# Four edits to the three cross-attention stages: the causal mask ahead of the scores, one eviction per half of P^T, the centring on ScalarE, the variance add on GpSimd

## The chip, the cores and the metric

One core of one Trainium2 chip. The metric is the device time of one execution in microseconds; lower is better. The program has one launch and no arithmetic on the host.

## The reference

The input x has 64 batches of 128 tokens by 128 features; a context has 77 tokens by 128 features for each batch. Four layers follow each other. The first three are cross-attentions with 16 heads of 8 features (the kernel calls them A0, A1 and A2); two of them have a feed-forward layer behind them (F0, F2). The fourth is self-attention with its own feed-forward layer (A3, F3). A cross-attention layer computes, for each batch:

```
q = x @ Wq (+ bq);  k = ctx @ Wk (+ bk);  v = ctx @ Wv (+ bv)      # 128x128, 77x128, 77x128
s[h] = q[h] @ k[h]^T                                              # 16 heads of 128x77
A0: s += -1e9 where key > query          (causal)
A1: s = s * side[h];  s += -3e38 where mask[h]    (weights and a mask of 128x77 a head, from DRAM)
A2: s += -1e20 where the key's mask is 0
p = softmax(s * scale);  o = p @ v;  t = x + o (A0) or x + o @ Wo + bo (A1, A2)
y = (t - mean(t)) / sqrt(var(t) + 1e-5) * gamma + beta
```

## The kernel before

**Stages and loops.** The stages run one after the other in the order A0, F0, A1, A2, F2, A3, F3 and hand their results over in DRAM. In A0, A1 and A2 each engine runs a loop of its own over the 64 batches, unrolled four times, and the engines meet through semaphores only. In one step of the loop an engine works on several batches at once: in step b it does the scores of batch b+1, the transposes and exponentials of batch b, the output of batch b-1, and the layer norm of batches b-2 and b-3. The order inside a step is written by hand, and an engine does its instructions strictly in that order; nothing overtakes a waiting one.

**A step on TensorE** (function `step` of `cross_tensor`): `scores(b+1)` (L659: four fp32 products over 32 rows each, for four heads at a time, into PSUM banks 0 to 3); in A0 then eight bf16 products that add the causal mask, each with a 64x64 corner of the identity as one operand (L667), in A2 four that add the key mask from `keybias` (L673). Then `attend(b-1)` (L702), `transpose_p(b, 0)` (L685: eight transposes of 128x77, four into bank 4 and four into bank 5), `back(b-1)` (L716), the projections of keys, values and queries of later batches (L639, L642, L633), the transpose of x (L629), and `transpose_p(b, 1)` (L685 again, into the same banks 4 and 5, so it waits until the first half was evicted). The projected keys and values share banks 0 and 1 with the scores (columns from 308 on).

**A step on ScalarE**: `keep_att` (L819), in A1 the exponential of the second half (L766), `keep_pT(b, 0)` (L772: two evictions of 77x512, one for each bank, each with its own semaphore count), the eviction of the keys (L781 in A0, L779 in A2; in A1 four that build the blocked keys directly, L787), of values, queries (L806) and x transposed (L794), an exponential (L766), `keep_pT(b, 1)` (L772 twice), an exponential.

**A step on VectorE** in A0 and A2: the row maxima of the scores (L863) and the subtraction (L868), for two halves; the mean and variance of batch b-3 (L943) between the first two; then the normalised output (L916, L923), the sum with the residual (L935), in A2 the key mask of batch b+2 (L906), and the statistics (L939). In A1 (`step_weighted`): the product of scores and weights for both halves (L876), the variance add of batch b-3 (L947), the mask of half 0 (L881), 1/denominator, the maxima of half 0 (L889), the normalised output, the values, the sum (L935), the mask of half 1 (L881), the statistics, the maxima of half 1 (L889), mean and variance (L943).

**A step on GpSimd** in A0 and A2: variance add (L1021), power -1/2 (L1026), the residual with bias (L1017), the centring and scaling z = (t - mean) * rstd (L1030), the blocked keys of batch b+2 (L1004), gamma (L1035) and beta (L1038). In A1: the subtraction of the maximum for half 1 of batch b (L1009), the power (L1026), the residual (L1017), the centring (L1030), the subtraction for half 0 of batch b+1 (L1009), gamma (L1035), beta (L1038).

SyncE alone issues DMAs. The tensors `p`, `kblk`, `att` and `side` are cut out of one large SBUF tensor, which the profile calls `sb_region`.

Of the kernel before, what the change touches and what calls it, by code (L numbers as in the profile page):

```python
# [29 lines left out]
T = 128  # L30
D = 128
C = 77
# [106 lines left out]
def build_layers(nc, a, out):  # L139
# [3 lines left out]
    with ExitStack() as ctx:  # L143
# [31 lines left out]
        causal = sb("causal", [T, 2 * C], BF16)  # L175
# [116 lines left out]
        rstd_s = slots("rstd", [T, 1])  # L292
        z_s = slots("z", [T, D])
# [49 lines left out]
        causal32, tri32 = wvo[:, 0:2 * C], wvo[:, 512:512 + HC * SEG]  # L343
        causal_loads = []
        for r in range(2):
            both = a["c_causal"].rearrange("(g i) (h k) -> i g h k", g=2, k=C)
            causal_loads.append((causal32[r * KH:(r + 1) * KH, :].rearrange("p (g k) -> p g k", k=C), both[:, :, 0, :]))
# [60 lines left out]
        pT_made = event("pT_made", CROSS, parts=4)  # L408
        pT_kept = event("pT_kept", CROSS, parts=4)
# [12 lines left out]
        rstd_made = event("rstd_made", CROSS)  # L422
        z_made = event("z_made", CROSS)
# [190 lines left out]
        def cross_tensor(pe, ph):  # L614
# [28 lines left out]

            def scores(b):
                if ph == "A0" and b.first:
                    pe.wait_ge(masks_made, 3)
# [8 lines left out]
                if (b + -1).exists:  # L655
                    pe.wait_ge(taken.sem(b + -1), taken.count(ph, b + -1, 1))
                for c in range(NQ):
                    rows = slice(32 * c, 32 * c + 32)
                    mm = nc.tensor.matmul(bank[c][:, 0:QC], qT_s[b.par][rows, :], kblk_s[b.par][rows, :],  # L659
                                          start=True, stop=(ph == "A1"), skip_group_check=(ph == "A0"))  # L660
                if ph == "A0":
                    for c in range(NQ):
                        for g in range(2):
                            r = (g + c) % 2
                            rows = slice(r * KH, (r + 1) * KH)
                            later = causal[rows, g * C:(g + 1) * C].unsqueeze(1).to_broadcast([KH, QH, C])
                            mm = nc.tensor.matmul(bank[c][g * KH:(g + 1) * KH, 0:QC], identb[rows, r * KH:(r + 1) * KH], later,  # L667
                                                  start=False, stop=True, skip_group_check=True)
# [1468 lines left out]
```

## Time and profile before

| what | value |
| --- | --- |
| time, median of 3 runs | 2447.12 us (2447.01 to 2448.53) |
| the profiled execution: time, span | 2447.01 us, 2445.2 us |
| TensorE / VectorE / GpSimd / ScalarE busy, share of the span | 93% / 77% / 64% / 62% |
| A0, first to last scores | 9.7 to 353.9 us |
| A1, first to last power | 543.8 to 922.7 us |
| A2, first to last key mask | 921.8 to 1271.1 us |

The profiled execution agrees with the median to 0.1 us. The span is what the trace covers; 1.8 us of the time lie around it. The three cross-attention stages have 192 steps in all. The page's shares are means over stages that have different limits, so the steady part of each stage is shown apart among the rows below.

### The profile page before, as it was taken

To read this page: it belongs to the slowest core of one execution; us is meant where nothing else is said; L and a number is where in the kernel's file an instruction comes from. 1 tells how busy PE (TensorE), PEld (TensorE's weight loads), DVE (VectorE), ACT (ScalarE), POOL (GpSimd) and SP (SyncE) were. 2 spreads that over 40 slices of the span, in tenths; PEclk is the share of its full clock that TensorE was granted. 3 is DMA by queue.
4 is the path that set the end of the run, shared out by engine and by line. 5 is a ranking of instruction groups with operands and counts; after the bars stand their busy time and mean duration, and the time that the engine had idled before them with its cause. 6 is when DMAs were issued, how large, how long until landed. Compare 5 with 4: busy or idle time off the path is not lost.

```text
span 2445.2 us, 84677 instructions
## 1 busy us (share of the span) xinstructions
PE 2268.4 (93%) x27182; PEld 1803.6 (74%) x27182; DVE 1876.9 (77%) x4067; ACT 1509.1 (62%) x3728; POOL 1555.4 (64%) x2374
## 2 busy tenths in 40 slices
PE   7999999988888888999999979999999999999899
PEld 5777778966666666777778867777777777777677
DVE  5888871159999986777775678888888888888565
ACT  5888884558888886888884524444444444444433
POOL 2666662229999994666667766666666666666332
PEclk9999999979999998999999999999999999999999
DMA  4111112235555542222221233333333333333111
GB/s 128 45 45 44 45 45 64 82 103 168 167 167 166 166 130 53 50 50 51 50 48 58 70 79 93 95 96 96 96 95 94 94 94 94 95 94 92 51 58 54
DMA packets 443189, 211.73 MB, mean 87 GB/s; under 512 B 206672, under 2 KB 434000, under 8 KB 442960
## 3 DMA queue, kind: packets, MB, share of 16 engines
q1 hardware_dynamic: 443088, 210.43, 31.9%
q8 instruction: 57, 0.93, 0.2%
q14 instruction: 44, 0.36, 0.1%
HBM read 113.28 MB, written 29.88 MB: 59 GB/s over the span
## 4 chain that ended last, share of the span: by engine, by line
PE 51%; POOL 18%; issue 16%; DVE 8%; SPq 3%; DMA 2%; ACT 1%; POOLq 1%; DVEq 0%; ACTq 0%
PE bank L1457 9%; PE bank L1417 9%; PE bank L1148 5%; POOL sb_region L1009 4%; PE bank L1485 4%; PE bank L659 4%; PE bank L1162 4%; POOL sb_rstd L1026 4%; POOL sb_z L1030 3%; PE bank L1467 3%; PE bank L1443 3%; DVE sb_max L863 2%; PE bank L685 2%; PE bank L1493 2%; POOL sb_region L1004 1%
## 5 line engine op out<-in xcount | busy, mean ns | idle before, releaser
L772 ACT ACTIVATE sb_pT<-bank 77x512 f32<-77x512 f32 x768 | 413.1, 591 | 19.5 <-PE bank L685 13.2
L685 PE MATMUL bank<-sb_ident,sb_region 128*77 128x128 f32 x3072 | 412.8, 278 | 5.3 <-ACT sb_pT L772 3.0
L685 PEld LDWEIGHTS bank<-sb_ident,sb_region 128*77 128x77 f32 x3072 | 355.1, 151 | 32.6 <-issue 14.4
L1547 ACT ACTIVATE sb_l<-sb_l 128x640 f32<-128x640 f32 x128 | 94.4, 738 | 388.0 <-DVE sb_l L1595 388.0
L863 DVE TENSOR_REDUCE sb_max<-bank 128x8 f32<-128x616 f32 x256 | 203.5, 795 | 128.5 <-PE bank L673 65.9
L766 ACT ACTIVATE sb_region<-sb_region 128x616 f32<-128x616 f32 x384 | 277.7, 724 | 21.3 <-POOL sb_region L1009 21.0
L1674 POOL TENSOR_TENSOR sb_pn<-sb_l,sb_r_all 128x512 f32<-128x512 f32 x128 | 134.7, 1052 | 234.2 <-DVE sb_r_all L1605 226.2
L1417 PE MATMUL bank<-sb_region,sb_wqkv 128*128 128x128 f32 x2048 | 253.3, 277 | 5.8 <-DVE sb_region L1583 5.0
L659 PE MATMUL bank<-sb_region,sb_qT 32*128 32x308 f32 x1536 | 158.1, 481 | 100.6 <-ACT sb_region L787 37.9
L1457 PE MATMUL bank<-sb_wvo,sb_region 128*64 128x512 f32 x1024 | 247.9, 605 | 0.0
L1417 PEld LDWEIGHTS bank<-sb_region,sb_wqkv 128*128 128x128 f32 x2048 | 241.7, 194 | 8.2 <-DVE sb_region L1583 5.7
L868 DVE TENSOR_TENSOR sb_region<-bank,sb_max 128x616 f32<-128x616 f32 x256 | 204.8, 800 | 18.5
L702 PE MATMUL bank<-sb_pT,sb_v 77*32 77x128 f32 x6144 | 209.0, 276 | 1.8 <-ACT sb_pT L772 1.8
L1665 POOL TENSOR_TENSOR sb_region<-sb_region 128x512 f32<-128x512 f32 x128 | 162.5, 1269 | 71.7 <-PE bank L1443 62.8
L702 PEld LDWEIGHTS bank<-sb_pT,sb_v 77*32 77x32 f32 x6144 | 155.7, 109 | 70.3 <-issue 57.2
L1009 POOL TENSOR_TENSOR sb_region<-sb_region,sb_max 128x616 f32<-128x616 f32 x128 | 174.5, 1364 | 37.0 <-DVE sb_max L889 37.0
L1485 PEld LDWEIGHTS bank<-sb_region,sb_pT 128*64 128x64 f32 x2048 | 121.6, 137 | 79.3 <-issue 67.3
L1197 ACT ACTIVATE sb_fh<-bank,sb_L_xattn_ffb 128x256 f32<-128x256 f32 x256 | 109.0, 472 | 112.6 <-PE bank L1148 112.6
L1531 ACT ACTIVATE sb_region<-bank 128x512 f32<-128x512 f32 x256 | 150.9, 592 | 40.1 <-PE bank L1457 31.0
L1583 DVE TENSOR_TENSOR sb_region<-bank,sb_sinT 128x512 f32<-128x512 f32 x256 | 174.3, 681 | 0.0
L1583 DVE TENSOR_TENSOR sb_region<-bank,sb_cosT 128x512 f32<-128x512 f32 x256 | 172.7, 675 | 1.4 <-PE bank L1417 1.3
L659 PEld LDWEIGHTS bank<-sb_region,sb_qT 32*128 32x128 f32 x1536 | 63.0, 187 | 144.2 <-issue 123.8
(181 smaller groups left out, 5531.9 us busy)
## 6 DMA issues: line engine op xcount, KB each, us to landing
sb_region<-in_side SPq DMA_DIRECT2D x64, 616.0 KB, 3.8
sb_pT<-sb_region SPq DMA_DIRECT2D x512, 64.0 KB, 2.0
sb_kF<-sb_region SPq DMA_DIRECT2D x512, 64.0 KB, 2.1
scratch_after_A<-sb_y SPq DMA_DIRECT2D x256, 64.0 KB, 1.8
sb_fx<-scratch_after_A SPq DMA_DIRECT2D x96, 128.0 KB, 2.1
sb_mask<-in_mask SPq DMA_DIRECT2D x64, 154.0 KB, 2.3
sb_x<-scratch_after_F SPq DMA_DIRECT2D x128, 64.0 KB, 1.9
sb_ctx<-in_ctxT SPq DMA_DIRECT2D x192, 38.5 KB, 1.8
```

Of the source, the lines that this page charges most:

```text
L659: mm = nc.tensor.matmul(bank[c][:, 0:QC], qT_s[b.par][rows, :], kblk_s[b.par][rows, :], start=True, stop=(ph == "A1"), skip_group_check=(p ...
L685: mm = nc.tensor.transpose(bank[4 + q][0:C, h * T:(h + 1) * T], p_s[b.par][:, head * C:(head + 1) * C], ident[:])
L702: mm = nc.tensor.matmul(att_bank[32 * i:32 * i + 32, k * T:(k + 1) * T], v_s[b.par][:, first:first + 32], pT_s[k][:, h * T:(h + 1) * T], s ...
L766: nc.scalar.activation(half(p_s[b.par], k), half(p_s[b.par], k), ACT.Exp, scale=SCALE[ph]).then_inc(exp_made.sem(b), 1)
L772: nc.scalar.activation(pT_s[k][:, q * QH * T:(q + 1) * QH * T], bank[4 + q][0:C, :], ACT.Copy).then_inc(pT_kept.sem(b), 1)
L863: nc.vector.tensor_reduce(dst, by_bank_and_head(scores_half(k)), AX.X, ALU.max).then_inc(max_made.sem(b), 1)
L868: nc.vector.tensor_tensor(by_bank_and_head(by_bank(half(p_s[b.par], k))), by_bank_and_head(scores_half(k)), spread_max(k), ALU.subtract).t ...
L1009: nc.gpsimd.tensor_tensor(by_head(half(p_s[b.par], k)), by_head(half(p_s[b.par], k)), spread(max_s[:, 8 * k:8 * k + 8], C), ALU.subtract)\
L1417: mm = nc.tensor.matmul(rope_bank[eo][:, n * T:(n + 1) * T], wqkv[:, col:col + 128], xnT_s[b.lap], start=True, stop=True)
L1457: mm = nc.tensor.matmul(vo_banks[g][r * SEG:(r + 1) * SEG, :], xnT_s[b.lap][:, g * SEG:(g + 1) * SEG], wvo[:, (2 * h + r) * HC * D:(2 * h ...
L1485: nc.tensor.matmul(out3_bank[g * SEG:(g + 1) * SEG, 0:D], pT_s3[h][:, c * T + g * SEG:c * T + (g + 1) * SEG], vo_s[h][:, (g * HC + c) * D: ...
L1583: ins = nc.vector.tensor_tensor(part[what][eo].rearrange("p (n t) -> p n t", t=T), src, table[:].unsqueeze(1).to_broadcast([128, BLOCKS, T ...
```

## The change

- **Causal mask (A0).** The mask tile grows from two 77-column blocks in 64-row parts to the full 128x308. The eight corner products behind the scores go. Four products of the full 128x128 identity with the full mask stand ahead of the scores in their PSUM banks (`start=True`), and the scores accumulate onto them. Those of banks 0 and 1 are issued at the end of the step before (`mask_early`), after waiting until the keys and values that share these banks were evicted; those of banks 2 and 3 stand right ahead of the scores, behind their waits.
- **P^T (A0, A1, A2).** The two evictions of 77x512 become one of 77x1024, over both banks. It waits for all eight transposes, and the second half's transposes wait for the whole of it.
- **Layer norm (A1).** VectorE's variance add (L947) goes; GpSimd does it (as in A0 and A2). GpSimd's centring goes; in its place GpSimd makes -mean * rstd of 128x1 (`scale_mean`), and ScalarE does z = t * rstd + shift of 128x128 between `keep_xT` and `keep_pT(b, 1)`.
- **Loads.** The causal mask is loaded by one DMA in place of two.

```diff
-        causal = sb("causal", [T, 2 * C], BF16)
+        causal = sb("causal", [T, QC], BF16)
...
+        shift_s = slots("mean_shift", [T, 1])
...
-        pT_made = event("pT_made", CROSS, parts=4)
-        pT_kept = event("pT_kept", CROSS, parts=4)
+        pT_made = event("pT_made", CROSS, parts=2)
+        pT_kept = event("pT_kept", CROSS, parts=2)
...
+            def mask_early(b, values):
+                if b.first:
+                    pe.wait_ge(masks_made, 3)
+                pe.wait_ge(k_kept.sem(b), k_kept.count(ph, b))
+                if values:
+                    pe.wait_ge(v_kept.sem(values), v_kept.count(ph, values))
+                for c in range(2):
+                    nc.tensor.matmul(bank[c][:, 0:QC], identb[:], causal[:], start=True, stop=False)
...
+                if ph == "A0":
+                    for c in range(2, NQ):
+                        nc.tensor.matmul(bank[c][:, 0:QC], identb[:], causal[:], start=True, stop=False)
                 for c in range(NQ):
                     rows = slice(32 * c, 32 * c + 32)
                     mm = nc.tensor.matmul(bank[c][:, 0:QC], qT_s[b.par][rows, :], kblk_s[b.par][rows, :],
-                                          start=True, stop=(ph == "A1"), skip_group_check=(ph == "A0"))
-                if ph == "A0":
-                    for c in range(NQ):
-                        for g in range(2):
-                            r = (g + c) % 2
-                            rows = slice(r * KH, (r + 1) * KH)
-                            later = causal[rows, g * C:(g + 1) * C].unsqueeze(1).to_broadcast([KH, QH, C])
-                            mm = nc.tensor.matmul(bank[c][g * KH:(g + 1) * KH, 0:QC], identb[rows, r * KH:(r + 1) * KH], later,
-                                                  start=False, stop=True, skip_group_check=True)
+                                          start=(ph != "A0"), stop=(ph != "A2"))
...
             def transpose_p(b, k):
                 pe.wait_ge(exp_made.sem(b), exp_made.count(ph, b, k))
-                for q in range(2):
-
-                    old, old_k = (b, 0) if k == 1 else (b + -1, 1)
-                    if old.exists:
-                        pe.wait_ge(pT_kept.sem(old), pT_kept.count(ph, old, 2 * old_k + q))
-                    for h in range(QH):
-                        head = (2 * k + q) * QH + h
-                        mm = nc.tensor.transpose(bank[4 + q][0:C, h * T:(h + 1) * T], p_s[b.par][:, head * C:(head + 1) * C], ident[:])
-                    mm.then_inc(pT_made.sem(b), 1)
+
+                if k == 1:
+                    pe.wait_ge(pT_kept.sem(b), pT_kept.count(ph, b, 0))
+                elif (b + -1).exists:
+                    pe.wait_ge(pT_kept.sem(b + -1), pT_kept.count(ph, b + -1, 1))
+                for h in range(2 * QH):
+                    head = k * 2 * QH + h
+                    mm = nc.tensor.transpose(two[0:C, h * T:(h + 1) * T], p_s[b.par][:, head * C:(head + 1) * C], ident[:])
+                mm.then_inc(pT_made.sem(b), 1)
...
                 if has(0):
                     transpose_p(b, 1)
+                if has(2) and ph == "A0":
+                    mask_early(b + 2, b + 1 if has(1) else None)
...
             def keep_pT(b, k):
+                act.wait_ge(pT_made.sem(b), pT_made.count(ph, b, k))
                 wait_earlier(act, att_made, ph, b, 1, k)
-                for q in range(2):
-                    act.wait_ge(pT_made.sem(b), pT_made.count(ph, b, 2 * k + q))
-                    nc.scalar.activation(pT_s[k][:, q * QH * T:(q + 1) * QH * T], bank[4 + q][0:C, :], ACT.Copy).then_inc(pT_kept.sem(b), 1)
+                nc.scalar.activation(pT_s[k][:], two[0:C, :], ACT.Copy).then_inc(pT_kept.sem(b), 1)
...
+            def centre(b):
+                act.wait_ge(mean_scaled.sem(b), mean_scaled.count(ph, b))
+                wait_earlier(act, zg_made, ph, b, 2)
+                nc.scalar.activation(z_s[b.par][:], t_s[b.par][:], ACT.Identity, bias=shift_s[b.par][:, 0:1], scale=rstd_s[b.par][:, 0:1])\
+                    .then_inc(z_made.sem(b), 1)
...
                     keep_xT(b + 3)
+                if has(-3) and weighted:
+                    centre(b + -3)
                 if has(1) and not weighted:
                     exps(b + 1, 0)
...
-                if has(-3):
-                    variance(b + -3)
-                if has(1):
                     mask(b + 1, 0)
...
+            def scale_mean(b):
+
+                nc.gpsimd.tensor_scalar(shift_s[b.par][:], mv_s[b.par][:, 0:1], rstd_s[b.par][:, 0:1], -1.0, ALU.mult, ALU.mult)\
+                    .then_inc(mean_scaled.sem(b), 1)
...
                     if has(-3):
-                        root(b + -3)
+                        rstd(b + -3)
+                        wait_earlier(pool, z_made, ph, b + -3, 2)
                     if has(-1):
                         residual(b + -1)
                     if has(-3):
-                        centre(b + -3)
+                        scale_mean(b + -3)
```

## Rows read from the trace of the kernel before

**Rows 1.** Busy time by stretch (steady A0, A1, A2): length, then PE, PEld, DVE, ACT, POOL.
```profile
99.58:322.45 222.87, 212.70 (x3066) 166.68 (x3067) 184.81 (x421) 189.38 (x464) 148.70 (x295) 1.00 0.17 45
570.00:880.00 310.00, 259.13 (x3409) 207.38 (x3412) 285.64 (x655) 273.58 (x707) 293.04 (x352) 1.00 0.57 167
963.82:1249.73 285.91, 266.63 (x3744) 221.96 (x3745) 226.62 (x521) 244.98 (x625) 183.97 (x365) 1.00 0.23 50
```
**Rows 2.** Timeline of a step of A0: start, length, engine, line, operation, [idle before <-releaser].
```profile
181.20 1.10 PE L685 MATMUL bank<-sb_ident,sb_region 128*77 128x128 f32 x8
181.90 1.08 ACT L772 ACTIVATE sb_pT<-bank 77x512 f32<-77x512 f32 x2 [0.18 <-PE bank L685]
182.98 0.91 PEld L685 LDWEIGHTS bank<-sb_ident,sb_region 128*77 128x77 f32 x8
...
183.53 0.70 POOL L1004 TENSOR_TENSOR sb_region<-sb_kT,sb_rowmask 128x308 f32<-128x308 f32 x1
184.46 0.80 PE L659 MATMUL bank<-sb_region,sb_qT 32*128 32x308 f32 x8 [0.33 <-POOL sb_region L1004]
185.19 0.47 PE L667 MATMUL bank<-sb_causal,sb_identb 64*64 64x308 bf16 x8
185.59 1.08 PE L702 MATMUL bank<-sb_pT,sb_v 77*32 77x128 f32 x32
```
**Rows 3.** Groups by line over the span: busy us, mean ns of one, idle before.
```profile
L772 ACT ACTIVATE sb_pT<-bank 77x512 f32<-77x512 f32 x768 | 413.1, 591 | 19.5 <-PE bank L685 13.2
L819 ACT ACTIVATE sb_region<-bank 128x256 f32<-128x256 f32 x192 | 73.6, 383 | 108.3 <-PE bank L702 108.3
L1021 POOL TENSOR_TENSOR sb_var<-sb_mv,sb_ln_eps 128x1 f32<-128x1 f32 x128 | 24.6, 192 | 183.8 <-DVE sb_mv L943 183.8
```
**Rows 4.** Timeline of a step of A1.
```profile
702.52 1.21 POOL L1009 TENSOR_TENSOR sb_region<-sb_region,sb_max 128x616 f32<-128x616 f32 x1
703.61 0.79 DVE L881 SCALAR_TENSOR_TENSOR sb_region<-sb_mask,sb_region 128x616 f32<-128x616 uint8 x1
703.76 0.72 ACT L766 ACTIVATE sb_region<-sb_region 128x616 f32<-128x616 f32 x1 [0.26 <-POOL sb_region L1009]
703.78 1.05 POOL L1026 TENSOR_TENSOR sb_rstd<-sb_var,sb_minus_half 128x1 f32<-128x1 f32 x1
705.49 0.80 POOL L1030 TENSOR_SCALAR sb_z<-sb_t,sb_mv,sb_rstd 128x128 f32<-128x128 f32 x1
705.91 0.79 DVE L881 SCALAR_TENSOR_TENSOR sb_region<-sb_mask,sb_region 128x616 f32<-128x616 uint8 x1
706.26 1.51 POOL L1009 TENSOR_TENSOR sb_region<-sb_region,sb_max 128x616 f32<-128x616 f32 x1
707.02 0.80 DVE L889 TENSOR_REDUCE sb_max<-sb_region 128x8 f32<-128x616 f32 x1
708.68 1.21 POOL L1009 TENSOR_TENSOR sb_region<-sb_region,sb_max 128x616 f32<-128x616 f32 x1
```
**Rows 5.** Instructions of line 1026: duration ns min/median/max, first and last start.
```profile
L1026 POOL TENSOR_TENSOR sb_rstd<-sb_var,sb_minus_half x192: 557/560/1123, 38.8 to 1289.2; 128x1 f32<-128x1 f32 x192
```
**Rows 6.** Timeline of VectorE and GpSimd at the start of A1.
```profile
533.29 1.22 POOL L1009 TENSOR_TENSOR sb_region<-sb_region,sb_max 128x616 f32<-128x616 f32 x1 [2.38 <-DVE sb_max L889]
533.52 1.65 DVE L881 SCALAR_TENSOR_TENSOR sb_region<-sb_mask,sb_region 128x616 f32<-128x616 uint8 x1
```
**Rows 7.** Timeline of a step of A2.
```profile
1103.30 1.04 PE L685 MATMUL bank<-sb_ident,sb_region 128*77 128x128 f32 x8
1104.99 0.24 ACT L779 ACTIVATE sb_kT<-bank 128x77 f32<-128x77 f32 x1
1105.46 0.70 POOL L1004 TENSOR_TENSOR sb_region<-sb_kT,sb_rowmask 128x308 f32<-128x308 f32 x1
1106.12 0.46 POOL L1035 TENSOR_TENSOR sb_zg<-sb_z,sb_L_xattn_ln_g 128x128 f32<-128x128 f32 x1
1106.19 0.44 DVE L906 TENSOR_SCALAR sb_keybias<-sb_keymask 128x77 bf16<-128x77 int32 x1
```

More of the change, by code:

```diff
@@ L341, in build_layers @@
         persK = sb("persK", [128, H // 2, NPM])
[L343 to L347, printed above, removed]
+        causal32, tri32 = wvo[:, 0:QC], wvo[:, 512:512 + HC * SEG]
+        causal_loads = [(causal32, a["c_causal"])]
         consts.append((tri32, a["c_tri"]))
@@ L422, in build_layers @@
         rstd_made = event("rstd_made", CROSS)
+        mean_scaled = event("mean_scaled", ["A1"])
         z_made = event("z_made", CROSS)
@@ L642, in project_values @@
                 nc.tensor.matmul(v_bank[0:C, V_COL:V_COL + D], ctx_s[b.par][:], w["wv"][:], start=True, stop=True).then_inc(v_made.sem(b), 1)
+            def mask_early(b, values):
[6 more added lines that the diff above has]
+                    nc.tensor.matmul(bank[c][:, 0:QC], identb[:], causal[:], start=True, stop=False)
             def scores(b):
-                if ph == "A0" and b.first:
-                    pe.wait_ge(masks_made, 3)
                 pe.wait_ge(kblk_made.sem(b), kblk_made.count(ph, b))
@@ L677, in transpose_p @@
                 pe.wait_ge(exp_made.sem(b), exp_made.count(ph, b, k))
[L678 to L686 removed]
+                if k == 1:
[6 more added lines that the diff above has]
+                mm.then_inc(pT_made.sem(b), 1)
             def attend(b, k, columns=None):
[L689 removed]
+                pe.wait_ge(pT_kept.sem(b), pT_kept.count(ph, b, k))
                 if k == 0:
@@ L856, in half_free @@
             def half_free(b, k):
-                wait_earlier(dve, pT_made, ph, b, 2, 2 * k + 1)
+                wait_earlier(dve, pT_made, ph, b, 2, k)
             def peak(b, k):
@@ L943, in aggregate @@
                 nc.vector.bn_aggr(mv_s[b.par][:], stats_s[b.par][:]).then_inc(mv_made.sem(b), 1)
-            def variance(b):
-                dve.wait_ge(mv_made.sem(b), mv_made.count(ph, b))
-                nc.vector.tensor_scalar(var_s[b.par][:], mv_s[b.par][:, 1:2], LN_EPS, None, ALU.add).then_inc(var_made.sem(b), 1)
             def step_weighted(b, has):
@@ L1021, in rstd @@
                 nc.gpsimd.tensor_tensor(var_s[b.par][:], mv_s[b.par][:, 1:2], ln_eps[:, 0:1], ALU.add).then_inc(var_made.sem(b), 1)
-                root(b)
-            def root(b):
                 pool.wait_ge(var_made.sem(b), var_made.count(ph, b))
@@ L2007, in _ @@
             nc.vector.tensor_copy(identb[:], ident[:]).then_inc(masks_made, 1)
-            dve.wait_ge(causal_loaded, 2 * 16)
+            dve.wait_ge(causal_loaded, 1 * 16)
             nc.vector.tensor_copy(causal[:], causal32).then_inc(masks_made, 1)
```

1 line of the change is left out of this document (removed).

## The prediction

> **What bounds the kernel now.** The page comes first, for the stages and the shares, then the busy time by stretch, then the timeline of one step of each stage, and last the groups by line for durations. Only A0, A1 and A2 run changed code, 64 steps each. In the stretches [rows 1] GpSimd has seven instructions in a step, so they hold 295/7 = 42, 352/7 = 50 and 365/7 = 52 steps, and a step takes 222.87/42 = 5.31 us in A0, 310/50.3 = 6.17 in A1 and 285.91/52 = 5.50 in A2. The reader is to see there that no stage is simply full: TensorE is 95% busy in A0, GpSimd 95% in A1, and in A2 TensorE shows 93% and VectorE 79%. The timeline tells what closes each step.
>
> In A0 the scores start 0.23 us after the blocked keys are done (184.46 against 183.53 + 0.70) and TensorE had stood idle for 0.33 by then [rows 2]. The loop is scores, mask, maxima, statistics, GpSimd's chain to the blocked keys, scores. TensorE's own work is close behind it.
>
> In A1 GpSimd looks full, but part of that is waiting. Its power takes 0.56 us at the median of the kernel and 1.05 here; its subtraction takes 1.21 at 702.52 and 1.51 at 706.26 [rows 4, 5]. Each long one lies over VectorE's mask (L881), and each ends a fixed time behind it: the power 0.43 after the mask that ends at 704.40, the subtraction 1.07 after the one that ends at 706.70. The other way round, a mask issued at 533.52 inside a subtraction that ends at 534.51 takes 1.65 and ends 0.66 after it [rows 6]. So these two kinds of instruction exclude each other, and who is issued first goes first. Written as a loop with M the end of the first mask: subtraction of half 1 ends 703.73, M = 704.40 (+0.67), second mask issued M+1.51, ended M+2.30, subtraction of half 0 ends M+3.37, gamma, beta and the next half-1 subtraction end 709.89 = M+5.49. 0.67 + 5.49 = 6.16, the step. The centring (0.80 at 705.49) is not in it: it lies beside the normalised output on VectorE and ends at 706.29, before the second mask lets go at 706.70.
>
> In A2 the scores wait for the key mask (L906), which ends at 1106.63, itself stretched to 0.44 over GpSimd's gamma product (1106.12 to 1106.58) [rows 7]. The blocked keys were done at 1106.16.
>
> **The change part by part: one eviction of P^T.** The evictions of 256 and 512 columns take 383 and 591 ns [rows 3], 0.81 ns a column, so 1024 columns take an estimated 1.01 us. Two evictions back to back take 1.08 [rows 2], so ScalarE gains 0.07 a half, which it doesn't need: it is busy 85 to 88% [rows 1]. Bounds for the new one are 0.90 and 1.08. What counts is when it starts and ends. With T the start of the first half's transposes (181.20), the first eviction starts at T+0.70, four transposes in; the other four take half of 0.91 more, so the joined one starts at T+1.16 and ends at T+2.17. The second half's transposes now wait for that and start at T+2.20, where they started at T+1.78.
>
> **A0.** TensorE's chain becomes: wait to T+2.20; eight transposes to the next instruction 1.0 (0.91 of weight loads and the first product's start); four full mask products; scores 0.73 (184.46 to 185.19); attend 1.0 to the next T. The old chain checks it: 184.46 + 0.73 + 0.40 + 1.01 gives 186.60, 5.40 after 181.20, in a step a little longer than the mean. A full bf16 product of 308 columns has no row. The eight corner products take 0.40, four of them at most side by side, so one round is 0.05 to 0.20; I take 0.13 each, 0.52 for four, and 0.40 to 0.80 as bounds. The sum is 2.20 + 1.0 + 0.52 + 0.73 + 1.01 = 5.46 against 5.31: +0.15 a step, **+10 us** over 64. The loop through the blocked keys does get shorter: only two products (0.26) stand between keys and scores where 0.40 stood behind them, so 5.31 - 0.14 = 5.17, but TensorE no longer reaches it. The keys' eviction (0.24 by A2's row [rows 7]) now ends near T+2.4, so the blocked keys run T+2.5 to T+3.2, 0.2 later than now; TensorE has its transposes and first two products behind it only at T+3.46. `mask_early` waits for keys and values that ScalarE evicts right behind T+2.17, before TensorE gets there at T+3.20: nothing. With both ends of the unknown costs A0 goes from -2 to +28; the upper end needs every product at its worst, so +18 is the end I keep.
>
> **A1.** VectorE loses its variance add, GpSimd loses 0.80 and gains a variance add (0.19 [rows 3]), a 128x1 product (about 0.2, by the same row) and their gaps. The first mask is still held until the half-1 subtraction ends, so M stays at +0.67, and VectorE's way from M to M+2.30 is untouched. GpSimd now does behind M: the rest of the variance add (0.1), the power 0.56, residual and gaps 0.66 (704.83 to 705.49 [rows 4]), the product 0.2: it issues the half-0 subtraction at M+1.5, where the second mask is issued at M+1.51. If the mask is first, the subtraction still ends at M+3.37 and the step stays 6.16: the freed 0.3 to 0.4 us turns into waiting for the mask. If the subtraction is first, it ends at M+2.71, the mask ends 0.66 behind it at M+3.37, the maxima at M+4.49 (1.12 behind the mask, 706.70 to 707.82), the next half-1 subtraction at M+5.77: the step is 6.44, +0.27. I take a third of the steps so: 21 x 0.27 = **+5 us**, with 0 and +17 as bounds. ScalarE's centring (370 ns at most, a 256-column copy takes 383 [rows 3]) stands behind the query eviction, where ScalarE has 12% free [rows 1] and gamma comes 1.5 us later; joined evictions pay for 0.14 of it: nothing. What is queued behind it, the second half's eviction and an exponential, moves by 0.2 and has a step's time to be used.
>
> The Trainium skill (SBUF — State Buffer, section on the two separate sides) says the SBUF port pair that VectorE and GpSimd share is an exclusive lock, taken for a whole instruction by whichever starts first, for a VectorE instruction with two SBUF inputs. The trace agrees: 1.65 us for a mask of 0.79 [rows 6]. By a rule of shared bandwidth instead, the centring's 0.80 would come off the step in part, and A1 would gain.
>
> **A2.** Here only the eviction changes. T is 1103.30; the joined eviction runs from T+1.16 to T+2.17 = 1105.47, the keys' eviction (0.24) ends near 1105.6 where it ended at 1105.23, the blocked keys run 1105.68 to 1106.38 where they ran 1105.46 to 1106.16. Scores at 1106.77 leave 0.2 for that. The key mask issued at 1106.19 then meets the blocked keys, not gamma, and gets through at 1106.45 in place of 1106.63: -0.18 where it goes so. In steps in which it is issued later it meets gamma, which is 0.2 later itself. I take -0.1 a step, **-6 us**; bounds are -11 and, if gamma always gets ahead of it, +12.
>
> Layer norm code elsewhere is untouched, and one larger mask load at the start (158 KB in place of twice 39) lies before the first scores: under 1 us, left out. The sum against the profiled execution (2447.0, 0.1 under the median): 2447 + 10 + 5 - 6 = **2456 us**.
>
> **The rivals.** (a) A1 is set free: GpSimd's 0.80 counts in full. Then ScalarE's chain bounds the step; its wait for the half-1 subtraction is 0.26 [rows 4], so at most 0.26 x 64 = 17 us come off: 2447 - 17 + 10 - 6 = 2434. For it speaks GpSimd's 95%; against it the subtraction's end 1.07 behind the mask. It decides when the half-0 subtraction ends well before M+3.3. (b) The second half's transposes aren't late, or the full mask products cost under 0.1 each, and A0 closes over the blocked keys at 5.17: -9, sum 2447 - 9 + 5 - 6 = 2437. Against it stands the start at T+2.20. (c) The subtraction wins every time in A1: 2447 + 10 + 17 - 6 = 2468. (d) A2's key mask doesn't profit, or is stuck behind gamma: 2447 + 10 + 5 + 0 to 12 = 2462 to 2474. (e) The edits cancel, A0's loss at half its size: 2450.
>
> **How the numbers follow.** Under 0.2% (4.9 us) a measurement can't tell this kernel from no change. Chances: forecast (2452 to 2461) 0.38; (a) 0.14; (b) 0.13; (c) 0.10; (d) 0.10; (e) 0.15. Faster by over 0.2%: (a) and nearly all of (b), 0.26. Within: (e) and the edges of (b) and of the forecast, 0.18. Slower: the rest, 0.56. The range takes 2436 to 2470: it leaves out most of (a) and the end of (d). The forecast's own range is 2452 to 2461.
>
> **What would show it.** In the new profile: one eviction of 77x1024 near 1.0 us; transposes of the second half 2.2 us behind those of the first in A0; no wait of TensorE for blocked keys there; a step of 5.46. In A1 power no longer stretched but the variance add is (to 0.7), masks of over 1.2 us in some steps, a step of 6.16 to 6.44. In A2 a key mask that ends right behind the blocked keys. The prediction is wrong if A1's step falls under 6.0, if TensorE still waits for the blocked keys in A0, or if A2's scores come to wait for them.

## The result and the profile after

The changed kernel takes 2475.32 us (2472.53 to 2476.01, 4 runs) against 2447.14 (2447.01 to 2448.53, 4 runs): the ratio is 1.0111, with a 95% interval of 1.0094 to 1.013. It is slower, as forecast, but by 28 us where 9 were forecast, and outside the range.

The span went from 2445.2 to 2470.1 us in the profiled execution, which took 2471.87 us, 3.4 less than the median. The starts of the scores say where the 24.9 us are. The table gives the mean step in us over 40 steps in the middle of each stage, taken between the starts of the scores on TensorE. The experiments below are in it too. The steps come from one profiled execution of each kernel, the ratios from all its timed ones.

| kernel | A0 | A1 | A2 | ratio to before (95%) |
| --- | --- | --- | --- | --- |
| before | 5.31 | 6.17 | 5.50 | |
| changed | 5.59 | 6.33 | 5.42 | 1.0111 (1.0094 to 1.013) |
| mask edit only | 5.30 | 6.18 | 5.50 | 1.0005 (0.9995 to 1.0015) |
| joined eviction only | 5.52 | 6.16 | 5.41 | 1.0040 (1.0025 to 1.0055) |
| norm edits only | 5.31 | 6.34 | 5.51 | 1.0058 (1.0038 to 1.0078) |
| changed, two evictions again | 5.29 | 6.33 | 5.51 | 1.0045 (1.0027 to 1.0062) |
| norm edits, product on VectorE | 5.31 | 6.24 | 5.50 | 1.0013 (1.0001 to 1.0025) |
| before, late blocked keys in A2 | 5.32 | 6.17 | 5.44 | 0.9992 (0.9975 to 1.0009) |
| before, four masks early | 5.12 | 6.17 | 5.50 | 0.9952 (0.9935 to 0.997) |
| before, other GpSimd order in A1 | 5.31 | 6.14 | 5.50 | 0.9992 (0.9982 to 1.0002) |
| changed, four masks early | 5.58 | 6.33 | 5.41 | 1.0108 (1.0093 to 1.0124) |
| combined | 5.12 | 6.18 | 5.45 | 0.9957 (0.9943 to 0.9971) |

From first to last scores (63 steps) A0 got 16.9 us longer (344.1 to 361.0), A1 8.2 (387.8 to 396.0), A2 3.9 shorter (345.9 to 342.0). The stretches between the stages, which hold the tail of one and the head of the next, add 2.3 (F0) and 1.3 (between A1 and A2). The sum is 24.8, the rest is at the two ends. By the ratios, the mask edit alone (+0.05%), the joined eviction alone (+0.40%) and the norm edits alone (+0.58%) add up to +1.03%, close to the +1.11% of the whole.

Busy time by stretch of the changed kernel, steady A0, A1 and A2, for [rows 1]; the columns are the same:

```profile
99.00:322.00 223.00, 212.29 (x2758) 165.08 (x2757) 177.18 (x401) 172.22 (x359) 143.68 (x280) 1.00 0.16 42
570.00:880.00 310.00, 260.13 (x3335) 200.16 (x3335) 291.87 (x591) 279.57 (x639) 287.40 (x393) 1.00 0.55 163
960.00:1250.00 290.00, 284.25 (x3826) 227.02 (x3827) 227.07 (x524) 235.71 (x531) 181.04 (x357) 0.99 0.24 52
```

In A1 GpSimd's busy share fell only from 95% to 93%, and VectorE's rose from 92% to 94%, although GpSimd lost 0.80 us of centring a step and VectorE lost an instruction: both now hold instructions that are stretched. In A2 TensorE went from 93% to 98%.

**A0, a step of the changed kernel**, timeline, for [rows 2]:

```profile
182.21 1.10 PE L686 MATMUL bank<-sb_ident,sb_region 128*77 128x128 f32 x8
...
183.35 1.02 ACT L774 ACTIVATE sb_pT<-bank 77x1024 f32<-77x1024 f32 x1 [0.54 <-PE bank L686]
...
184.51 1.07 PE L686 MATMUL bank<-sb_ident,sb_region 128*77 128x128 f32 x8 [0.25 <-ACT sb_pT L774]
...
184.66 0.70 POOL L1007 TENSOR_TENSOR sb_region<-sb_kT,sb_rowmask 128x308 f32<-128x308 f32 x1 [0.21 <-ACT sb_kT L783]
...
185.42 0.42 PE L650 MATMUL bank<-sb_causal,sb_identb 128*128 128x308 bf16 x2
...
185.68 0.42 PE L665 MATMUL bank<-sb_causal,sb_identb 128*128 128x308 bf16 x2
...
186.03 0.80 PE L668 MATMUL bank<-sb_region,sb_qT 32*128 32x308 f32 x8
...
```

T, the start of the first half's transposes, is 182.21. The joined eviction runs from T+1.14 to T+2.16, the second half's transposes start at T+2.30, and TensorE names the eviction as what it waited for. In the kernel before, the last products ahead of them and the transposes were these:

```profile
182.98 0.27 PE L629 MATMUL bank<-sb_ident,sb_x 128*128 128x128 f32 x1
183.09 1.04 PE L685 MATMUL bank<-sb_ident,sb_region 128*77 128x128 f32 x8
```

There T is 181.20. The transposes stood at T+1.89, right behind the work in front of them and with no wait: the two evictions had begun with four transposes still to come and had both ended by T+1.78 [rows 2]. In the changed kernel the four mask products take 0.61 (185.42 to 186.03). The blocked keys are done at 185.36, and TensorE shows no wait for them any more.

**A1**, a step of the changed kernel, for [rows 4]:

```profile
707.02 0.75 POOL L1024 TENSOR_TENSOR sb_var<-sb_mv,sb_ln_eps 128x1 f32<-128x1 f32 x1
707.85 0.55 POOL L1026 TENSOR_TENSOR sb_rstd<-sb_var,sb_minus_half 128x1 f32<-128x1 f32 x1
708.72 0.45 POOL L1020 TENSOR_TENSOR sb_xb<-sb_xr,sb_L_xattn_bo 128x128 f32<-128x128 f32 x1 [0.32 <-POOL sb_rstd L1026]
709.15 0.91 POOL L1035 TENSOR_SCALAR sb_mean_shift<-sb_mv,sb_rstd 128x1 f32<-128x1 f32 x1
710.03 1.21 POOL L1012 TENSOR_TENSOR sb_region<-sb_region,sb_max 128x616 f32<-128x616 f32 x1
```
```profile
706.71 1.01 DVE L891 SCALAR_TENSOR_TENSOR sb_region<-sb_mask,sb_region 128x616 f32<-128x616 uint8 x1
...
709.15 0.79 DVE L891 SCALAR_TENSOR_TENSOR sb_region<-sb_mask,sb_region 128x616 f32<-128x616 uint8 x1
```

The variance add takes 0.75 in place of 0.19 [rows 3] and ends 0.05 behind the first mask (707.72). The product of one element a partition, issued at 709.15 with the second mask, takes 0.91 and ends 0.12 behind it. The half-0 subtraction is no longer stretched, but it starts only then and ends 1.30 behind the mask where it ended 1.07 behind it. With M the end of the first mask, as in the prediction, its end is M+3.52 in place of M+3.37.

**A2**, a step of the changed kernel, for [rows 7]:

```profile
1115.20 1.02 ACT L774 ACTIVATE sb_pT<-bank 77x1024 f32<-77x1024 f32 x1 [0.47 <-PE bank L686]
...
1116.36 1.07 PE L686 MATMUL bank<-sb_ident,sb_region 128*77 128x128 f32 x8
1116.50 0.70 POOL L1007 TENSOR_TENSOR sb_region<-sb_kT,sb_rowmask 128x308 f32<-128x308 f32 x1 [0.34 <-ACT sb_kT L781]
1116.84 0.42 DVE L916 TENSOR_SCALAR sb_keybias<-sb_keymask 128x77 bf16<-128x77 int32 x1
...
1117.47 0.80 PE L668 MATMUL bank<-sb_region,sb_qT 32*128 32x308 f32 x8
```

The key mask is stretched over the blocked keys and gets through 0.06 behind them. The scores start with no wait for it shown, right behind the second half's transposes. Those start 0.14 behind the joined eviction (1116.22), so that in this stage too TensorE now follows the eviction.

### The profile page after: what moved, and what is told of

Its sections match the earlier page's. It is cut to its first block, busy times and chain, and to the rows that moved or that the text cites. A ratio compares the mean times of both kernels' runs of the same rounds, so it can differ in the third digit from the quotient of the medians.

```text
span 2470.1 us, 83369 instructions
## 1 busy us (share of the span) xinstructions
PE 2308.8 (93%) x26926; PEld 1812.7 (73%) x26926; DVE 1888.0 (76%) x4003; ACT 1498.6 (61%) x3408; POOL 1559.2 (63%) x2438
## 4 chain that ended last, share of the span: by engine, by line
PE 68%; POOL 16%; issue 6%; ACT 3%; DVE 3%; DMA 2%; SPq 1%; POOLq 1%; DVEq 0%; ACTq 0%
PE bank L686 10%; PE bank L1463 9%; PE bank L1423 9%; POOL sb_region L1012 5%; PE bank L703 5%; PE bank L1491 5%; PE bank L1154 4%; PE bank L668 4%; PE bank L1168 4%; PE bank L1473 3%; PE bank L1449 3%; ACT sb_pT L774 3%; POOL sb_mean_shift L1035 2%; POOL sb_var L1024 2%; PE bank L1499 2%
## 5 line engine op out<-in xcount | busy, mean ns | idle before, releaser
L774 ACT ACTIVATE sb_pT<-bank 77x1024 f32<-77x1024 f32 x384 | 391.6, 1020 | 81.4 <-PE bank L686 80.4
L686 PEld LDWEIGHTS bank<-sb_ident,sb_region 128*77 128x77 f32 x3072 | 348.3, 151 | 112.1 <-issue 108.2
L769 ACT ACTIVATE sb_region<-sb_region 128x616 f32<-128x616 f32 x384 | 276.9, 722 | 25.0 <-POOL sb_region L1012 24.9
L703 PE MATMUL bank<-sb_pT,sb_v 77*32 77x128 f32 x6144 | 216.2, 277 | 3.8 <-ACT sb_pT L774 3.6
L1012 POOL TENSOR_TENSOR sb_region<-sb_region,sb_max 128x616 f32<-128x616 f32 x128 | 158.8, 1241 | 37.5 <-DVE sb_max L899 37.5
L1024 POOL TENSOR_TENSOR sb_var<-sb_mv,sb_ln_eps 128x1 f32<-128x1 f32 x192 | 68.0, 354 | 174.8 <-DVE sb_mv L953 174.8
```

What stands on the lines that cost most here:

```text
L686: mm = nc.tensor.transpose(two[0:C, h * T:(h + 1) * T], p_s[b.par][:, head * C:(head + 1) * C], ident[:])
L703: mm = nc.tensor.matmul(att_bank[32 * i:32 * i + 32, k * T:(k + 1) * T], v_s[b.par][:, first:first + 32], pT_s[k][:, h * T:(h + 1) * T], s ...
L769: nc.scalar.activation(half(p_s[b.par], k), half(p_s[b.par], k), ACT.Exp, scale=SCALE[ph]).then_inc(exp_made.sem(b), 1)
L774: nc.scalar.activation(pT_s[k][:], two[0:C, :], ACT.Copy).then_inc(pT_kept.sem(b), 1)
L1012: nc.gpsimd.tensor_tensor(by_head(half(p_s[b.par], k)), by_head(half(p_s[b.par], k)), spread(max_s[:, 8 * k:8 * k + 8], C), ALU.subtract)\
```

## The experiments

**Mask edit only.** The kernel before with the causal-mask part of the diff.

```diff
+                for c in range(2):       # mask_early, end of the step before
+                    nc.tensor.matmul(bank[c][:, 0:QC], identb[:], causal[:], start=True, stop=False)
...
+                    for c in range(2, NQ):       # in scores, behind its waits
+                        nc.tensor.matmul(bank[c][:, 0:QC], identb[:], causal[:], start=True, stop=False)
```

> The kernel before with the causal-mask edit alone (A0). Theory: A0's loss in the changed kernel comes from the second half's transposes starting 0.5 us late, and the four full mask products (0.61 us in the changed kernel, 0.40 for the eight corner products) hurt only because they stand behind that delay. Alone, the mask edit takes 0.14 us out of the loop through the blocked keys and leaves TensorE's chain at 1.78 + 0.91 + 0.11 + 0.61 + 0.73 + 1.01 = 5.15: A0 at 5.15 to 5.2 us a step against 5.31, the whole at 2438 to 2441. Rival: the mask products themselves are what slows A0; then this kernel has most of the 0.27 us a step, some 2460.

Measured: 2449.3 against 2448.41 us, ratio 1.0005; A0 at 5.30. The rival falls: the mask edit doesn't slow A0. The expected gain isn't there either. Timeline of a step:

```profile
182.78 0.70 POOL L1005 TENSOR_TENSOR sb_region<-sb_kT,sb_rowmask 128x308 f32<-128x308 f32 x1
...
183.19 0.42 PE L648 MATMUL bank<-sb_causal,sb_identb 128*128 128x308 bf16 x2
...
183.71 0.43 PE L663 MATMUL bank<-sb_causal,sb_identb 128*128 128x308 bf16 x2
...
184.07 0.80 PE L666 MATMUL bank<-sb_region,sb_qT 32*128 32x308 f32 x8
...
184.94 0.80 DVE L864 TENSOR_REDUCE sb_max<-bank 128x8 f32<-128x616 f32 x1 [0.97 <-PE bank L666]
```

From the end of the blocked keys (183.48) to the maxima it is 1.46 us. In the kernel before, the blocked keys end at 184.23 [rows 2], and the maxima start 1.47 later:

```profile
185.70 0.80 DVE L863 TENSOR_REDUCE sb_max<-bank 128x8 f32<-128x616 f32 x1 [0.98 <-PE bank L667]
```

The two late full products take 0.36 (183.71 to 184.07), and the maxima start 0.87 behind the start of the scores, which are now last. Before, the scores took 0.73 until the corner products, and the maxima started 0.51 behind the start of those. 0.36 + 0.87 is 1.23, 0.73 + 0.51 is 1.24. Nothing is gained.

**Joined eviction only.** The kernel before with one eviction of 77x1024.

```diff
-                for q in range(2):
-                    act.wait_ge(pT_made.sem(b), pT_made.count(ph, b, 2 * k + q))
-                    nc.scalar.activation(pT_s[k][:, q * QH * T:(q + 1) * QH * T], bank[4 + q][0:C, :], ACT.Copy)...
+                act.wait_ge(pT_made.sem(b), pT_made.count(ph, b, k))
+                nc.scalar.activation(pT_s[k][:], two[0:C, :], ACT.Copy)...
```

> The kernel before with the joined eviction alone (A0, A1, A2). Theory: A0 takes 5.40 to 5.50 a step (the blocked keys are 0.1 to 0.2 later and the corner masks still stand behind the scores), +6 to +12 us; A1 is unchanged, because GpSimd and the masks on VectorE close its step; A2 falls to 5.42 as in the changed kernel, -5 us. Sum 2448 to 2454. Rival: A1's extra 0.16 us a step is the joined eviction's too; then A1 is at 6.33 and the sum is 10 us higher, 2458 to 2464.

Measured: 2457.24 against 2448.41 us, ratio 1.0040; A0 5.52, A1 6.16, A2 5.41. The rival falls: A1's loss isn't the eviction's. A0 loses 0.21 a step here already, a little more than the 0.10 to 0.20 expected. All of A2's gain is here. In A0 the mask edit, which costs nothing alone, adds 0.07 a step to this (5.52 to 5.59 in the changed kernel): there the two edits do interact. TensorE's chain is the longer one once the eviction is late, and four full mask products take 0.61 in it where the corner products took 0.40, while the transposes take 0.91 to the next instruction in place of 1.00.

**Norm edits only.** The kernel before with A1's layer-norm edits.

```diff
-                    variance(b + -3)              # VectorE
...
-                        centre(b + -3)            # GpSimd
+                        rstd(b + -3)              # GpSimd, with the variance add
...
+                        scale_mean(b + -3)        # GpSimd, 128x1
...
+                    centre(b + -3)                # ScalarE
```

> The kernel before with the layer-norm edits of A1 alone. Theory: all of A1's loss is here (half-0 subtraction on GpSimd getting in ahead of the second mask on VectorE): A1 at 6.3 us a step against 6.17, +8 to +12 us, 2456 to 2459; A0 and A2 as before. Rival 1: the loss is the joined eviction's, and this kernel is at 2447 or below. Rival 2: GpSimd's freed time counts without the longer eviction, and A1 falls under 6.1: 2440.

Measured: 2459.92 against 2448.41 us, ratio 1.0058; A1 at 6.34, A0 and A2 as before. All of A1's loss is here. How it comes about differs between the start of A1 and its steady part. At the start, GpSimd and then VectorE:

```profile
540.86 0.26 POOL L1035 TENSOR_SCALAR sb_mean_shift<-sb_mv,sb_rstd 128x1 f32<-128x1 f32 x1
541.08 1.21 POOL L1012 TENSOR_TENSOR sb_region<-sb_region,sb_max 128x616 f32<-128x616 f32 x1
```
```profile
541.27 1.68 DVE L891 SCALAR_TENSOR_TENSOR sb_region<-sb_mask,sb_region 128x616 f32<-128x616 uint8 x1
```

The product takes 0.26, the subtraction gets in ahead of the mask, and the mask takes 1.68. The next half-1 subtractions start at 544.06 and 550.30: a step of 6.24. From the fifth product on (566.21) to the one at 882.81, it is the product that waits for the mask, with 0.91 to 1.08 us each, at 6.34 a step. One of them, GpSimd and then VectorE:

```profile
705.44 1.04 POOL L1035 TENSOR_SCALAR sb_mean_shift<-sb_mv,sb_rstd 128x1 f32<-128x1 f32 x1
706.44 1.21 POOL L1012 TENSOR_TENSOR sb_region<-sb_region,sb_max 128x616 f32<-128x616 f32 x1
```
```profile
705.64 0.79 DVE L891 SCALAR_TENSOR_TENSOR sb_region<-sb_mask,sb_region 128x616 f32<-128x616 uint8 x1
```

The product starts 0.20 before the mask in the records, and still ends 0.05 behind it, while the mask keeps its 0.79. So for this pair the record that starts first is not the one that goes first. In this trace every product that starts 0.25 us or more ahead of the mask takes 0.25 to 0.27, and each one that starts up to 0.24 ahead of it waits. The prediction had only the first of the two outcomes as a loss, and took the second for free.

**The changed kernel with two evictions.** Everything but the joined eviction.

```diff
-                act.wait_ge(pT_made.sem(b), pT_made.count(ph, b, k))
...
-                nc.scalar.activation(pT_s[k][:], two[0:C, :], ACT.Copy).then_inc(pT_kept.sem(b), 1)
+                for q in range(2):
+                    act.wait_ge(pT_made.sem(b), pT_made.count(ph, b, 2 * k + q))
+                    nc.scalar.activation(pT_s[k][:, q * QH * T:(q + 1) * QH * T], bank[4 + q][0:C, :], ACT.Copy)...
```

> The changed kernel with P^T evicted in two halves again. Theory: the parts add up by stage: A0 as with the mask alone (5.15 to 5.2), A1 as with the norm edits alone (6.3), A2 as before (5.50): 2447 - 7 + 10 = 2450. Rival: the edits interact in A1 (the centring on ScalarE hurts only beside the longer eviction), and this kernel is at 2440.

Measured: 2458.06 against 2448.41 us, ratio 1.0045 (+10 us where +3 was expected by sum); A0 5.29, A1 6.33, A2 5.51. Stage by stage it is the mask-only and the norm-only kernel side by side, so the edits don't interact in A1. Its time is 8 us above the expected 2450. The expectation had 7 us for a gain of the mask edit, and that gain isn't there. In the trace the stretches between stages are also longer than in the kernel before (behind A0 164.1 against 162.7 us, behind A1 23.2 against 21.6), but that execution took 2465.91 us, the longest of four, so this is only an indication.

**Norm edits with the product on VectorE.** The diff is against the kernel with the norm edits only.

```diff
-                        scale_mean(b + -3)        # GpSimd, between residual and subtraction
+                if has(-3):
+                    scale_mean(b + -3)            # VectorE, between values and sum
```

> The norm edits of A1 alone, with the 128x1 product of mean and rstd made by VectorE (between the values and the sum) and not by GpSimd. In the norm-only kernel that product is issued on GpSimd within 0.05 us of VectorE's second mask, loses, takes 0.9 to 1.1 us in place of 0.26, and the half-0 subtraction starts only behind it, 0.1 behind the mask's end, with its full 1.21. Theory: A1's step is set by the turns that masks and GpSimd's two-input instructions take. Without the product GpSimd issues the subtraction ahead of the mask, the mask is stretched to about 1.65, and the step is 6.2 to 6.25, as in the first steps of A1 in the norm-only kernel (6.24): still not under 6.17, although GpSimd now does 0.8 us less than before. Rival: A1's loss is the product's 0.7 us of GpSimd time; without it A1 falls under 6.1.

Measured: 2452.6 against 2448.54 us, ratio 1.0013; A1 at 6.24. A step of GpSimd and then VectorE at 700 us:

```profile
700.39 1.22 POOL L1020 TENSOR_TENSOR sb_region<-sb_region,sb_max 128x616 f32<-128x616 f32 x1
702.30 0.45 POOL L1043 TENSOR_TENSOR sb_zg<-sb_z,sb_L_xattn_ln_g 128x128 f32<-128x128 f32 x1 [0.70 <-ACT sb_z L820]
```
```profile
700.94 1.32 DVE L891 SCALAR_TENSOR_TENSOR sb_region<-sb_mask,sb_region 128x616 f32<-128x616 uint8 x1
```

The subtraction is first now (700.39 against 700.94) and the mask takes 1.32. GpSimd stands idle for 0.70 us before gamma, and the stage is still not faster than with the whole centring on GpSimd. The rival falls: GpSimd's work was not what bound A1. Of the 0.17 a step that the norm edits cost, 0.10 goes with the product's place on GpSimd. Which of the other norm edits costs the remaining 0.07 was not tried apart.

**Late blocked keys in A2.** Nothing is removed; a wait is added.

```diff
+                if ph == "A2" and (b + -1).exists:       # block_keys, GpSimd
+                    pool.wait_ge(v_kept.sem(b + -1), v_kept.count(ph, b + -1))
```

> The kernel before; only in A2 GpSimd's blocked keys wait for the values' eviction too, which delays them by about 0.15 us and removes nothing. Theory: A2's gain in the changed kernel (5.50 to 5.41 a step) comes from the blocked keys being late, so that VectorE's key mask meets them and not the gamma product, and gets through right behind them. Then the late keys alone bring A2 to 5.35 to 5.43. Rival: the gain is ScalarE's, from one eviction in place of two; then this kernel stays at 5.50 or gets slower.

Measured: 2444.84 against 2448.54 us, ratio 0.9992, an interval that includes 1; A2 at 5.44 against 5.50, just outside what was expected and on the theory's side. Timeline of GpSimd, VectorE and TensorE:

```profile
1104.93 0.70 POOL L1006 TENSOR_TENSOR sb_region<-sb_kT,sb_rowmask 128x308 f32<-128x308 f32 x1 [0.22 <-ACT sb_v L813]
1105.41 0.28 DVE L906 TENSOR_SCALAR sb_keybias<-sb_keymask 128x77 bf16<-128x77 int32 x1
1105.86 0.80 PE L659 MATMUL bank<-sb_region,sb_qT 32*128 32x308 f32 x8 [0.25 <-DVE sb_keybias L906]
```

The key mask gets through 0.06 behind the blocked keys. The stage gets 0.06 us a step shorter by a wait alone; the joined eviction alone has 0.09. So the late keys account for most of A2's gain; that they account for all of it isn't shown.

**Four masks early.** The kernel before with all four mask products in `mask_early`. The diff is against the kernel with the mask edit only.

```diff
+                if values:
+                    pe.wait_ge(taken.sem(values), taken.count(ph, values, 1))
-                for c in range(2):
+                for c in range(NQ):
                     nc.tensor.matmul(bank[c][:, 0:QC], identb[:], causal[:], start=True, stop=False)
...
-                    for c in range(2, NQ):       # in scores
-                        nc.tensor.matmul(bank[c][:, 0:QC], identb[:], causal[:], start=True, stop=False)
```

> The kernel before with all four full causal-mask products of A0 at the end of the step before (the mask-only kernel has two of them there and two behind the wait for the blocked keys). Theory: the mask-only kernel gained nothing (5.30 a step) because its two late products cost 0.36 us and the scores' tail 0.07 between the blocked keys and the maxima, against 0.40 for the eight corner products. With all four early that is gone from the loop, and TensorE's own chain binds: 0.73 + 1.01 + 1.03 + 0.95 + 0.87 + 0.52 = 5.11: A0 at 5.1 to 5.15, -10 to -12 us. Rival: full mask products slow TensorE itself; then A0 stays at 5.3 or rises.

Measured: 2439.1 against 2448.54 us, ratio 0.9952 (0.9935 to 0.997): faster by 9.4 us where 10 to 12 were expected; A0 at 5.12. Timeline of TensorE:

```profile
182.68 1.10 PE L683 MATMUL bank<-sb_ident,sb_region 128*77 128x128 f32 x8
...
184.57 1.04 PE L683 MATMUL bank<-sb_ident,sb_region 128*77 128x128 f32 x8
...
185.44 0.69 PE L650 MATMUL bank<-sb_causal,sb_identb 128*128 128x308 bf16 x4
...
186.06 0.80 PE L665 MATMUL bank<-sb_region,sb_qT 32*128 32x308 f32 x8
```

T is 182.68. The second half starts at T+1.89, then come 0.87 of transposes, 0.62 of masks, and 0.73 + 1.01 as before: 5.12. It is TensorE's own chain, with no wait in it. The 0.62 is more than the 0.52 in the expected sum, which had the transposes between at 0.08 more.

**Another order on GpSimd in A1.** The same work, with gamma and beta one batch later, for which GpSimd's loop in A1 gets one more step at its end.

```diff
-                        centre(b + -3)
-                        shift(b + 1, 0)
-                        affine(b + -3)
+                        gamma(b + -4)
+                        centre(b + -3)
+                        beta(b + -4)
+                        shift(b + 1, 0)
```

> The kernel before; in A1 GpSimd does the gamma and beta of a batch one step later, around the centring and ahead of the half-0 subtraction: half-1 subtraction, power, residual, gamma, centring, beta, half-0 subtraction. The work is the same. Theory: A1's loop is a chain of turns (first mask, second mask, half-0 subtraction, gamma, beta, half-1 subtraction). Gamma fits between the masks, the centring lies over the second mask, and beta, the two subtractions and 0.66 for the first mask follow: 2.28 + 0.4 + 1.2 + 1.2 + 0.66 = 5.75, under which ScalarE's and TensorE's chain binds at some 5.9: A1 at 5.85 to 5.95 against 6.17, -14 to -20 us. Rival: GpSimd is simply full with 5.9 us of work a step; then the order changes nothing, 6.15 to 6.2.

Measured: 2446.58 against 2448.54 us, ratio 0.9992; A1 at 6.14. The expected 5.85 to 5.95 failed. A1 is 1.7 us shorter from first to last scores, and the stretch behind it is 4.3 us longer. The half-0 subtraction is now late, and ScalarE, which works in order, waits for it before the output's eviction:

```profile
708.43 0.72 ACT L766 ACTIVATE sb_region<-sb_region 128x616 f32<-128x616 f32 x1 [0.69 <-POOL sb_region L1009]
709.05 0.36 ACT L819 ACTIVATE sb_region<-bank 128x256 f32<-128x256 f32 x1
```
```profile
710.85 0.26 DVE L916 RECIPROCAL sb_rden<-bank 128x16 f32<-128x16 f32 x1 [0.56 <-PE bank L728]
```

VectorE then waits 0.56 us for the output on its way from the first mask to the second. This chain runs over four engines, and it was no faster than the old one. That the order of GpSimd alone can free A1 isn't shown.

**The changed kernel with four masks early.**

```diff
-                for c in range(2):
+                for c in range(NQ):      # mask_early of the changed kernel; it also waits for `taken`, and the two late ones go
```

> The changed kernel with the two late causal-mask products moved to the end of the step before as well. With the joined eviction kept, theory says that A0's step is TensorE's chain from the first half's transposes: 2.30 until the second half's start, 0.91 of transposes, 0.52 of masks in one piece, 0.73 scores, 1.01 attend = 5.47 to 5.50, against 5.58 in the changed kernel; the other 0.35 to the kernel with two evictions and four early masks (5.12) is the late start. Rival: the step is set by the blocked keys, which are late behind the joined eviction; they end 0.2 us before the late masks are done, and moving those masks would then bring A0 to 5.25.

Measured: 2474.41 against 2447.99 us, ratio 1.0108; A0 at 5.58, as in the changed kernel. The rival falls: the blocked keys don't set this step. Four masks take 0.62 in one piece and 0.61 in two, so the expected 5.47 was 0.10 too low for the same reason as the prediction's 5.46.

```profile
182.11 1.10 PE L685 MATMUL bank<-sb_ident,sb_region 128*77 128x128 f32 x8
...
184.41 1.07 PE L685 MATMUL bank<-sb_ident,sb_region 128*77 128x128 f32 x8 [0.25 <-ACT sb_pT L773]
...
185.31 0.69 PE L652 MATMUL bank<-sb_causal,sb_identb 128*128 128x308 bf16 x4
...
185.93 0.80 PE L667 MATMUL bank<-sb_region,sb_qT 32*128 32x308 f32 x8
```

Beside the kernel before with four masks early it is a pair that differs in A0 by the joined eviction alone: the second half starts at T+2.30 (T is 182.11) against T+1.89, and a step is 5.58 against 5.12.

**Combined.** Four masks early, joined eviction in A2 alone, A1 as before.

```diff
+        JOINED = ('A2',)        # one eviction of 77x1024 in these stages, two of 77x512 elsewhere
```

> The edits that paid, put together: all four causal-mask products early (A0), the joined eviction in A2 alone, A1 as before. Theory: stages add up: A0 5.12, A1 6.17, A2 5.41 a step, so 12 + 0 + 6 = 18 us off the kernel before, 2429 to 2432, ratio 0.993. Rival: what one stage gains comes back as a wait in the stage behind it, and the ratio stays above 0.996.

Measured: 2438.56 against 2447.99 us, ratio 0.9957 (0.9943 to 0.9971): faster than the kernel before by 9 us where 18 were expected, and so faster than the changed kernel too. A0 has its 5.12, but from first to last scores it is only 7.1 us shorter (337.0 against 344.1): the gain of 0.19 a step isn't there in its first ten steps, which take 65.1 us against 63.2 in the kernel before. A2 has 5.45, a smaller gain than the joined eviction alone had (5.41); why was not found. Four masks early alone had 0.9952, so the joined eviction in A2 adds nothing that can be measured.

## Why the prediction was wrong in size

**The sign and the places were right.** A0 and A1 lose, A2 gains, by the mechanisms named: late transposes, turns between masks and GpSimd, a key mask that meets another instruction. The forecast by stage was +10, +5 and -6 us; measured from first to last scores it is +17, +8 and -4, and 3.6 more between the stages. Each stage is inside the bounds that the prediction gave for it (-2 to +18, 0 to +17, -11 to +12). The whole lies outside the range because all three came out on the slow side of their forecasts at once, and because the stretches between them weren't in the sum. The last 3.4 us are the difference between the profiled execution and the median, and no trace places them.

**The step that failed is A0's sum, "2.20 + 1.0 + 0.52 + 0.73 + 1.01 = 5.46".** Measured it is 2.30 + 0.91 + 0.61 + 0.73 + 1.01 = 5.56 in most steps and 5.65 in every fourth, a mean of 5.59. The mechanism was right, and the term that was mis-sized is the mask products: 0.52 for four, at 0.13 each, from a span of 0.05 to 0.20 for which no row decided. They take 0.61, at 0.15 each, and these 0.09 are nearly the whole difference from 5.46. Two other terms were off and cancel. The second half's start was put 0.10 too early: the eviction was sized right (1.02 against 1.01), but TensorE's first product comes 0.14 behind its end. The transposes were put 0.09 too long. In every fourth step the eviction itself starts 0.07 later, at T+1.21 (172.22 with T at 171.01); what delays it was not found. (The lower bound of -2 doesn't follow from the bounds of the masks, 0.40 to 0.80: with them alone it is +2 to +28.) The kept upper end of +18 held the measured +17. That the joined eviction carries most of the loss is shown by the pair with four masks early (5.12 and 5.58) and by the eviction alone (5.52); the other 0.07 comes from the mask edit on top of it.

**The shorter loop through the blocked keys, "5.31 - 0.14 = 5.17", was wrong, though it didn't enter the sum.** The mask edit alone left A0 at 5.30. Two full products cost 0.36 and not 0.26, and from the start of the last group of products to the maxima it is 0.87 with the scores last and 0.51 with the corner products last. So rival (b) had no basis.

**In A1 the step that failed is "if the mask is first ... the step stays 6.16".** The race at M+1.5 was seen, but it was put between the mask and the half-0 subtraction, and the product was taken as 0.2 us that end before it. In the steady part the product of one element a partition was at the point of the race. It waited for the mask (0.91 to 1.08 us in place of 0.26), and the subtraction could only start behind it: 6.39 in two steps of four, 6.36 and 6.16 in the others. The reading behind the race, "who is issued first goes first", doesn't hold for the product either, which waits even when its record starts up to 0.24 us ahead of the mask's. The other outcome, the subtraction first, costs 0.07 (6.24 in the kernel with the product on VectorE and at the start of A1 in the norm-only one), not the 0.27 of the prediction. So +5 came from the wrong one of the two outcomes, and that it lies near the +8 measured is luck. Rival (c), +17, overshoots the +8 to +10 measured; rival (a), A1 set free, is refuted: the norm edits alone and the kernel with an idle GpSimd are both slower than 6.17.

**A2** went nearly as forecast (5.50 to 5.42, -0.08 against -0.1), and the late keys alone show the cause for most of it: -0.06. In the changed kernel TensorE is 98% busy there and its scores wait for nothing that the profile shows, so that little more was to be had from the key mask.

**Left out were the stretches between the stages.** The 3.6 us there weren't priced at all. The joined eviction alone has 1.0 of the 2.3 behind A0. The norm edits alone have a stretch there that is 3.2 us shorter (159.5 against 162.7), so it moves either way with what stands around it. Its cause stays open.

## What to carry to other kernels

Two evictions in a row also overlap with the engine that fills the banks: the first can start when the first bank is full. Joining them saved ScalarE 0.06 us and delayed TensorE's second half by 0.41, because the one eviction could start only behind all eight transposes and ended 0.38 later than the two had (T+2.16 against T+1.78). Before work is moved off an engine that looks full, look at which of its instructions are stretched and by what: in A1 the centring ran beside the mask at no cost, and the two small instructions that took its place on GpSimd, the variance add and the product, took turns with masks. And when work is put ahead of a wait, put all of it there: two of four mask products early gave nothing, four gave 0.5%.

## What the runs showed of the hardware that was not expected

- A GpSimd product of one element a partition with two scalar operands from SBUF takes 0.26 us alone and 0.91 to 1.08 when VectorE's mask starts with it or up to 0.25 us behind it; it then ends 0.04 to 0.14 behind the mask (norm edits only, and the changed kernel). The centring, of the same kind over 128 elements, overlaps such a mask by 0.38 us with both at their usual length (0.80 and 0.79 [rows 4]). The Trainium skill (SBUF — State Buffer, section on the two separate sides) has whoever starts first hold the shared pair for the whole instruction; for the centring, which starts first, this trace doesn't show that, and for the product the one that starts first in the records is not the one that goes first.
- An eviction of 77x1024 from two banks takes 1.02 us, two of 77x512 back to back 1.08. The slope of 0.81 ns a column from 256 and 512 columns [rows 3] gives 1.01 for 1024.
- Four full bf16 products of 128x128 with 308 columns take 0.61 to 0.62 us, eight with 64x64 corners 0.40.
